# A state-space step's scaled inputs formed on GpSimd, its decay products in half-width matmuls, and one sum issued earlier on VectorE

## What is computed

```python
q = (x * dw1) @ pw1 + b1;  v = (x * dw2) @ pw2 + b2
x = softmax(q @ q.T) @ v * gamma + x                    # per image, 1024 x 1024 scores

xn = rmsnorm(layernorm(x));  z, xBC, dt = split(xn @ W_in.T)
xBC = silu(causal_conv4(xBC) + conv_b);  dt = softplus(dt + dt_bias)
state = state * exp(dt * -exp(A_log)) + (dt * xs) B     # 8 heads of 32, 32 states, token by token
y = state . C + Dp * xs
t = x + (layernorm(x) + rmsnorm(y * silu(z)) @ W_out.T)

out = t + top2_moe(layernorm(t))                        # 8 experts, hidden 341, silu(h1) * h3
```

## Time and profile before

| | us |
|---|---|
| median of 3 runs | 1157.73 (1153.94 to 1158.94) |
| the profiled execution | 1154.58 |
| its span | 1152.8 |
| TensorE busy | 1047.1 (91%) |
| VectorE busy | 819.1 (71%) |
| ScalarE busy | 760.6 (66%) |
| GpSimd busy | 648.7 (56%) |

### The profile page before, as it was taken

The page is one execution under the profiler, slowest core; times in us unless marked ns, Lnnn a source line. Parts: engine busy times, 40 slices in busy tenths (PEclk is TensorE's granted clock), DMA queues, the critical chain, the costliest instruction groups (busy, mean ns, idle before and its releaser), DMA issues.

```text
span 1152.8 us, 27912 instructions
## 1 busy us (share of the span) xinstructions
PE 1047.1 (91%) x7924; PEld 955.6 (83%) x7924; DVE 819.1 (71%) x2766; ACT 760.6 (66%) x1914; POOL 648.7 (56%) x998
## 2 busy tenths in 40 slices
PE   4889999999999999999999999888889999999993
PEld 3778888888887878888888788777788999999983
DVE  3587878977988887897798888778535554444564
ACT  2677677777767867777777776667557666666552
POOL 8124453467557557646755756754765466444442
PEclk8999999999999999999999999989989999999997
DMA  7300000001000100100100000011112222223566
GB/s 214 74 3 30 11 3 30 7 26 41 14 26 9 41 21 12 48 7 26 41 12 28 9 24 11 16 44 27 42 54 64 64 80 78 80 73 89 182 185 188
DMA packets 66403, 58.64 MB, mean 51 GB/s; under 512 B 12869, under 2 KB 56429, under 8 KB 66253
## 3 DMA queue, kind: packets, MB, share of 16 engines
q1 hardware_dynamic: 48237, 34.54, 11.2%
q0 software_dynamic: 8704, 17.97, 4.6%
q10 hardware_dynamic: 9312, 4.33, 1.3%
HBM read 32.67 MB, written 25.21 MB: 50 GB/s over the span
## 4 chain that ended last, share of the span: by engine, by line
PE 49%; POOL 17%; issue 16%; DVE 9%; ACT 4%; DMA 3%; SPq 1%; ACTq 0%; DVEq 0%; POOLq 0%
PE pY L695 7%; PE pX L690 7%; PE pc L524 5%; PE pa L579 4%; POOL rows_by_expert L1173 3%; PE pd L707 3%; PE pb L707 3%; POOL RY L1128 3%; DVE CV L1457 2%; PE pY L488 2%; DMA GX<-rows_by_expert 2%; POOL YG L1111 2%; PE pc L528 1%; PE pX L429 1%; POOL st L1154 1%
## 5 line engine op out<-in xcount | busy, mean ns | idle before, releaser
L1062 POOL DMA_INDIRECT results_by_choice<-YE,DIX x144 | 144.1, 1001 | 146.6 <-ACT YE L953 118.7
L1173 POOL DMA_INDIRECT rows_by_expert<-XA,SL x128 | 148.0, 1157 | 34.8 <-issue 33.0
L1694 DVE TENSOR_TENSOR V<-XT,pY 128x384 f32<-128x384 f32 x132 | 73.1, 554 | 125.2 <-ACT XT L943 117.0
L1457 DVE SCALAR_TENSOR_TENSOR CV<-XBC,cw,CV 128x256 f32<-128x256 f32 x288 | 137.2, 530 | 0.1
L524 PEld LDWEIGHTS pc<-XDT,M 128*128 128x128 f32 x1024 | 124.6, 193 | 7.9 <-issue 3.3
L579 PE MATMUL pa<-V,PT 128*128 128x128 f32 x1024 | 128.3, 279 | 0.6 <-DVE XDT L1504 0.6
L1111 POOL TENSOR_TENSOR YG<-Y,SZ 128x256 f32<-128x256 f32 x64 | 46.4, 726 | 140.7 <-DVE Y L1493 136.2
L524 PE MATMUL pc<-XDT,M 128*128 128x64 f32 x1024 | 122.4, 273 | 2.4 <-DVE CT L1463 2.4
L579 PEld LDWEIGHTS pa<-V,PT 128*128 128x128 f32 x1024 | 120.6, 193 | 3.1 <-issue 1.0
L1468 DVE TENSOR_REDUCE NM<-pX 128x1 f32<-128x1024 f32 x64 | 78.1, 1220 | 54.4 <-PE pX L503 54.3
L935 ACT ACTIVATE XT<-pa 128x128 f32<-128x128 f32 x132 | 36.5, 277 | 105.5 <-PE pa L681 104.6
(11 more groups left out here) (315 smaller groups left out, 3035.2 us busy)
## 6 DMA issues: line engine op xcount, KB each, us to landing
GX<-rows_by_expert SPq DMA_DIRECT2D x144, 65.0 KB, 1.9
XT<-in_xT_dram SPq DMA_DIRECT2D x8, 512.0 KB, 4.3
X<-in_x_dram SPq DMA_DIRECT2D x16, 256.0 KB, 3.0
out_dram<-T ACTq DMA_DIRECT2D x16, 256.0 KB, 3.0
results_by_choice<-YE,DIX POOLq DMA_INDIRECT x144
rows_by_expert<-XA,SL POOLq DMA_INDIRECT x128, 2.5
XBC<-results_by_choice SPq DMA_DIRECT2D x8, 256.0 KB, 4.1
XA<-results_by_choice SPq DMA_DIRECT2D x8, 256.0 KB, 5.0
```

Of the source, the lines that this page charges most:

```text
L1062: g.indirect_dma_start(yg, bass.IndirectOffsetOnAxis(ap=DIX[:, slot, :], axis=0), YE[:, slot, :], None).then_inc(s(f"ye{slot}_scattered"), 16)
L1173: g.indirect_dma_start(xg, bass.IndirectOffsetOnAxis(ap=SL[:, j // NT, j % NT:j % NT + 1], axis=0), XA[:, j // NT, j % NT, :], None).then_ ...
L1457: return stt(CV[:, m, :], XBC[:, m, fo + tap:fo + tap + 256], cw[:, m, tap:tap + 1], CV[:, m, :], ALU.mult, ALU.add)
L1694: tt(HT[par].rearrange("p k t -> p (k t)"), SH[:, par, :], pY[:, 512 * par:512 * par + HP3], ALU.mult).then_inc(s("hh_ready"), 1)
```

## The change

XDT leaves VectorE. ScalarE copies the transposed inputs out of `pa` into a new SBUF tile XS, ahead of its copies of B and of C times B; GpSimd multiplies XS by DT, behind YG and ahead of XW. TensorE's L579 no longer waits for `xdt_ready`. The decay product of each head becomes two matmuls of 64 query columns each and 32 moving columns. And in odd steps Y2 is computed ahead of the third tap in place of behind it; in even steps it stays where it was.

```diff
--- before.py
+++ after.py
@@ -99,7 +99,7 @@
         CT3, NCT3 = sb("CT3", [P, 2, P], bf16), sb("NCT3", [P, 2, 2, P], bf16)
 
         XDT = sb("XDT", [P, 2, DI + HD])
-        XW, YO, Y2 = (sb(n, [P, DI]) for n in ("XW", "YO", "Y2"))
+        XS, XW, YO, Y2 = (sb(n, [P, DI]) for n in ("XS", "XW", "YO", "Y2"))
         YG = sb("YG", [P, DI])
         BNAT, GT = sb("BNAT", [P, P]), sb("GT", [P, P])
         ED, M = sb("ED", [P, H, P]), sb("M", [P, H, P])
@@ -521,7 +521,9 @@
                     if decays:
                         upto(pe, "cum1", base, d + 2)
                     for h in range(H):
-                        mm(pc[:, 64 * h:64 * h + 64], M[:, h, :], XDT[:, e % 2, HD * h:HD * h + 64], start=h == 0, stop=False, skip_group_check=True)
+                        for u in range(2):
+                            queries = slice(HP * u, HP * u + HP)
+                            mm(pc[queries, 64 * h:64 * h + HD], M[:, h, queries], XDT[:, e % 2, HD * h:HD * h + HD], start=h == 0, stop=False, skip_group_check=True)
 
                     y_heads = pc[:].rearrange("p (h w) -> p h w", h=H)
                     for m in range(2):
@@ -572,7 +574,6 @@
                 if there(base, o):
 
                     upto(pe, "pt_act", base, o + 1)
-                    upto(pe, "xdt_ready", base, k + 1)
                     upto(pe, "gT_ready", base, k + 1)
                     upto(pe, "t_ready", base, o)
                     for j in range(NT):
@@ -829,6 +830,8 @@
                     A(CTP[0:NS, kpar, :], SX[NS:2 * NS, kpar, 2, :], ACT.Copy).then_inc(s("bc_ready"), 2)
                 if there(base, k):
                     upto(act, "xs_ready", base, k + 1)
+                    upto(act, "xdt_ready", base, k)
+                    A(XS[:], pa[:, 0:DI], ACT.Copy).then_inc(s("xs_copied"), 1)
                     upto(act, "state_ps", base, k)
                     A(BNAT[:], pa[:, 2 * P:3 * P], ACT.Copy).then_inc(s("bnat_ready"), 1)
                     upto(act, "m_ready", base, k)
@@ -1111,6 +1114,11 @@
                     g.tensor_tensor(YG[:], Y2[:], SZ[:, (base + e) // 2 % 3, e % 2, :], ALU.mult).then_inc(s("yg_ready"), 1)
                 scatters(0)
                 if there(base, k):
+                    upto(pool, "xs_copied", base, k + 1)
+                    upto(pool, "dt_ready", base, k + 1)
+                    upto(pool, "ydiag_ps", base, k - 1)
+                    apart(pool)
+                    g.tensor_tensor(v3(XDT[:, k % 2, :]), v3(XS), b3(DT), ALU.mult).then_inc(s("xdt_ready"), 1)
                     upto(pool, "xdt_ready", base, k + 1)
                     upto(pool, "dec_exp", base, k + 1)
                     upto(pool, "state_ps", base, k)
@@ -1466,6 +1474,16 @@
                     upto(dve, "s_ready", base, i + 1)
                     upto(dve, "exp_ready", base, i - NT + 1)
                     v.tensor_reduce(NM[:, i:i + 1], pX[:], AX.X, ALU.max, negate=True).then_inc(s("nm_ready"), 1)
+                if i % 2 == 1 and there(base, e):
+                    upto(dve, "ydiag_ps", base, e + 1)
+                    upto(dve, "yg_ready", base, e)
+                    y_heads = pc[:].rearrange("p (h w) -> p h w", h=H)[:, :, 0:HD]
+                    if e % NT != 0:
+                        upto(dve, "yo_ready", base, e + 1)
+                        last = tt(v3(Y2), y_heads, v3(YO), ALU.add)
+                    else:
+                        last = v.tensor_copy(v3(Y2), y_heads)
+                    last.then_inc(s("y2_ready"), 1)
                 if decays:
                     upto(dve, "cv_evac", base, d + 2)
                     for m in range(3):
@@ -1484,7 +1502,7 @@
                         ts(XR[:, (fb + j) % NT, :], bank[:, DI + H:DI + H + E], st[:, fpar, 6, j:j + 1], st[:, fpar, 6, 2 + j:3 + j], ALU.mult, ALU.mult)
                         tt(dts[:, 0, j, :], bank[:, DI:DI + H], hrow[:, 0, :], ALU.add).then_inc(s("u_ready"), 1)
 
-                if there(base, e):
+                if i % 2 == 0 and there(base, e):
                     upto(dve, "ydiag_ps", base, e + 1)
                     upto(dve, "yg_ready", base, e)
                     y_heads = pc[:].rearrange("p (h w) -> p h w", h=H)[:, :, 0:HD]
@@ -1497,11 +1515,6 @@
                 if front_b:
                     upto(dve, "u_ready", base, fb + 2)
                     stt(dts[:, 1], dts[:, 0], -1.0, dts[:, 0], ALU.mult, ALU.min).then_inc(s("nau_ready"), 2)
-                if there(base, k):
-                    upto(dve, "gT_ready", base, k + 1)
-                    upto(dve, "xw_ready", base, k - 1)
-                    upto(dve, "ydiag_ps", base, k - 1)
-                    tt(v3(XDT[:, k % 2, :]), v3(pa), b3(DT), ALU.mult).then_inc(s("xdt_ready"), 1)
                 if i == 3 and routes:
                     rows(b)
                 if base == 0 and i == 5:
```

## The result

The changed kernel takes 1170.08 us (median of 4, 1169.0 to 1172.16), the kernel before 1156.14 on the same chip: a ratio of 1.0123, 95% interval 1.0105 to 1.0140. That is slower, inside the range and 6.5 us above the forecast of 1163.6: the change was to cost 5.9 us and costs 13.9 by the medians. The profiled execution took 1170.36 us with a span of 1168.6, 15.8 more than the span before. The sign was forecast, but most of the time is lost in two places that the forecast had priced at nothing or as gains.

What follows compares the result with a forecast made beforehand. TensorE sets the pace, with small holes ahead of L563. Per image -0.36, -0.04, +0.1, +0.3 and +1.1 make +1.1, over seven images +7.7; last steps -1.8; total +5.9, so 1160.5, by the median 1163.6 us; range 1148 to 1180.

Steps and rivals of the forecast that it cites:

- the mechanism that it held likeliest: A little slower, through GpSimd's list with XDT in steps 6, 7 and 0: 1163.6 us, chance 0.45.
- The product, 1.1 us: TensorE's decay product in halves takes 1.1 us in place of 1.73, between bounds of 1.07 and 1.93.
- the forecast's pace: A matmul's pace in the product follows its weight columns: 0.108 us for 128, 0.054 for 64.
- halves do not pay: Rival: the product takes 1.93 us, costing 3.6 us per image, 1183 us in all; chance 0.13.
- In even steps, nothing: Even steps keep their length, since VectorE's row up to Y2 is untouched, unless the product takes over about 1.8 us.
- Between -0.4 and +0.6: Step 3 into 4, set by VectorE: +0.1 us per image, between tap undisturbed (-0.4) and product at 1.73 (+0.6).
- ScalarE's floor: Odd steps: with XS, ScalarE ends YT at +5.93, L602 starts at +6.05; step 5 gains 0.36 us, step 1 0.04.
- Steps 7 and 0: XDT in GpSimd's list makes L1226 1.35 us later: step 7 loses 0.3 us per image, step 0 about 1.1.
- The last steps: Between expert matmuls, three odd steps with TensorE alone on the product's path gain 0.6 us each: -1.8 (0 to -3.6).
- steps 1, 5 and 6: Per image, step 1 gains 0.04 us and step 5 0.36; the sum gives step 6 no term of its own.

Runs made afterwards that it cites:

- x_only: XDT moved to GpSimd through ScalarE's copy, with whole matmuls and Y2 behind the tap, against the kernel before: 1159.82 us, ratio 1.0034.
- xdt_behind_tap: The changed kernel with Y2 behind the tap in the late steps and, in odd steps, GpSimd's XDT waiting for the third tap: 1163.92 us, ratio 1.0061.
- mixed: ahead_in_5 with XDT left on VectorE in step 7: 1145.8 us, ratio 0.9897 to the kernel before.
- ahead_in_5: The changed kernel with Y2 ahead of the tap in step 5 of each image alone, behind it elsewhere: 1148.54 us, ratio 0.9923.

## Why the prediction was right, and where it was wrong

Its sign and its range came true; the mechanism that it held likeliest did not carry the loss, and that the total fell into the range is in part luck.

- **The product, 1.1 us.** Right within 0.1: 1.05 from L526 to L530. The changeover is 0.10 ahead of it (575.89 to 575.99) and 0.05 behind (L530 to L537 takes 0.55, L528 to L535 took 0.50), 1.20 in all. The Trainium skill's page "TensorEngine Tiling (Array Packing)" (Key Properties) says that tiles load in parallel and that a change of mode drains the engine. The trace agrees with the first: one after the other, the forecast's pace gives 1.73. Of the second it shows 0.15 us lost around each product, and not that this is a drain. By the rival "halves do not pay" the product took 1.93. It is out.
- **"In even steps, nothing": failed.** Step 2 grew by 0.55 and step 4 by 0.74. The forecast followed TensorE from L563 on. It never worked out when VectorE leaves step 1, and for the end of step 3 it took no more than +0.1.
- **"Between -0.4 and +0.6" for step 3 to 4: right in its bounds, +0.52 for both steps, but its value of +0.1 was too low,** and the same sum was owed in step 1. "YG and XDT on GpSimd now run beside its tap" stood in the text and got no price of its own. It measures 0.83 in steps 1 and 5 (2.10 for 1.27) and 2.0 in step 7 (3.27 for 1.27). In step 3 the tap had been stretched to 1.67 before, and is 2.10 now. The contention was priced in the other direction only, GpSimd held up by M.
- **ScalarE's floor, L602 at +6.05 and YT's end at +5.93: right.** YT ends at +5.84, the output's line L603 starts at 581.77, +5.88, and step 5 is 0.43 shorter (forecast 0.36). x_only agrees that the floor depends on the halves.
- **Steps 7 and 0, "+0.3" and "+1.1", the largest term: failed in size.** Measured -0.17 and +0.49, 0.32 for both in place of 1.4. The forecast had VectorE's first operation behind the norm (LG) 1.35 later; in the step shown below it is at +7.94 for +7.61, 0.33 later. YG came at +2.79, not +3.5, and VectorE's wait for rs is 0.24, not 2. GpSimd's short operations ahead of YG tell why, after and then before:

```profile
551.86 0.19 POOL L1164 TENSOR_SCALAR st<-st 128x2 f32<-128x2 f32 x1 [0.20 <-POOL st L1162]
552.01 0.20 POOL L1165 TENSOR_TENSOR st<-st 128x2 f32<-128x2 f32 x1
552.17 0.20 POOL L1166 TENSOR_TENSOR st<-st,NMN 128x4 f32<-128x4 f32 x1
552.32 0.60 POOL L1105 TENSOR_TENSOR STE<-ST,ETOT 32x256 f32<-32x256 f32 x1
552.89 0.71 POOL L1114 TENSOR_TENSOR YG<-Y,SZ 128x256 f32<-128x256 f32 x1
```

```profile
549.57 0.42 POOL L1156 TENSOR_SCALAR st<-st 128x2 f32<-128x2 f32 x1 [0.20 <-POOL st L1154]
549.96 0.43 POOL L1157 TENSOR_TENSOR st<-st 128x2 f32<-128x2 f32 x1
550.36 0.44 POOL L1158 TENSOR_TENSOR st<-st,NMN 128x4 f32<-128x4 f32 x1
```

  Before, they ran beside VectorE's tap at over twice their length. Now VectorE waits for the product at that moment, and they are quick. And M starts at +6.48, not at +5.74, behind the first norm operations, since the tap ahead of it takes 3.27 beside GpSimd's list (DVE, the same step 7):

```profile
552.35 3.27 DVE L1465 SCALAR_TENSOR_TENSOR CV<-XBC,cw,CV 128x256 f32<-128x256 f32 x3
...
556.58 1.23 DVE L1580 TENSOR_TENSOR M<-ED,GT 128x1024 f32<-128x1024 f32 x1
558.04 0.23 DVE L1234 TENSOR_TENSOR LG<-LR,rs 128x64 f32<-128x64 f32 x1 [0.24 <-POOL rs L1085]
```

  The mechanism itself is real: a delayed XDT lengthens step 0 by 1.67 in xdt_behind_tap, and XDT by itself by 0.34 (13.71 in mixed, 14.05 in ahead_in_5).
- **The last steps, "-1.8 (0 to -3.6)": failed, with the wrong sign.** They measure +9.2. "TensorE alone on the path for the product" held, but the forecast looked only at the product and not at what stands behind Y2 on VectorE: tap, gated tile, an expert's matmul. That is 9.2 us beyond the worse of its bounds, 0, and 11.0 from its value, the largest error.

By the forecast's own count of seven images: steps 7 and 0 were to lose 9.8 and lost 2.2; steps 2 to 4 were to lose 0.7 and lost 7.5; steps 1, 5 and 6 were to gain 2.8 and gained 4.7; the late part was to gain 1.8 and lost 9.2. Step 4 of the last image adds 1.9. So two errors of 7.6 and 6.8 us with opposite signs cancelled within the total.

## What to carry to other kernels

Before an operation that waits is put ahead of one that doesn't, write down what each engine does during that wait and who waits for what now stands behind it, in every stage in which the code is used. Here, 27.2 us of work moved from VectorE to GpSimd came back as 27.4 us of stretch where the two then ran side by side on operands in SBUF: look at the pair's timing, and try a wait on the engine that has slack. Judge the parts of a change in pairs: the halves alone gave 0.25%, XDT alone lost 0.34%, both together gained 0.67%, and the third part lost 1.9% on top.

## What the runs showed of the hardware

- VectorE's tap (two operands in SBUF) takes 1.27 us for its three operations with GpSimd idle, 1.74 beside GpSimd's YG, and 2.10 beside YG and XDT. GpSimd's operations stretch too: YG from 0.72 to 0.90, XDT from 0.61 to 0.79, short ones from 0.19 to 0.43. The page "SBUF — State Buffer" of the Trainium skill (SBUF: two separate sides) describes an exclusive lock: whoever starts first holds the pair of ports for its whole instruction, and the other one is blocked. One after the other the three would take 1.27 + 0.72 + 0.61 = 2.60; they took 2.10. The direction agrees; by the durations shown here the overlap was not all lost.
- Thirty-two matmul instructions with 64 weight columns and 32 moving ones take 1.05 us where sixteen with 128 and 64 took 1.73. The sum of the weight columns is the same in both, and so is that of the moving columns, so neither count alone explains the gain. Whether the weights' side sets the pace, as the forecast assumed, these runs do not show.
- TensorE waited 3.19 us for V in the late part, and in the 5 us from the next matmul on the granted clock stood at 0.50 (1.2 GHz), with TensorE busy for 4.73 of them.
